# Ranking edges with one node range and a fifth of the edges on each partition, in a graph layer on one core

## The reference

```
edge_in = concatenate([h[row], h[col], dist], axis=1)
e   = silu(silu(edge_in @ eW1 + eb1) @ eW2 + eb2)
agg = segment_sum(e, row, num_segments=h.shape[0])
out = silu(concatenate([h, agg], axis=1) @ nW1 + nb1) @ nW2 + nb2
x   = layernorm(x + out)
```

## Time and profile before

| | |
|---|---|
| median of 3 runs | 629.42 us (627.53 to 630.96) |
| the profiled execution | 630.7 us, of which the span from the first to the last instruction is 628.9 us |
| busy: PE / PEld / DVE / ACT / POOL | 533.6 / 449.0 / 462.9 / 355.5 / 430.5 us |
| mean granted TensorE clock | 0.960 of full speed |

### The profile page before, as it was taken

The page is one execution under the profiler, slowest core; times in us unless marked ns, Lnnn a source line. Parts: engine busy times, 40 slices in busy tenths (PEclk is TensorE's granted clock), DMA queues, the critical chain, the costliest instruction groups (busy, mean ns, idle before and its releaser), DMA issues.

```text
span 628.9 us, 15166 instructions
## 1 busy us (share of the span) xinstructions
PE 533.6 (85%) x4653; PEld 449.0 (71%) x4653; DVE 462.9 (74%) x1364; ACT 355.5 (57%) x812; POOL 430.5 (68%) x465
## 2 busy tenths in 40 slices
PE   3953979779889979999998899889997888879695
PEld 2432768758768868887787788778776777769584
DVE  5998999988999898999788868797642533223356
ACT  4852555535645656665555555565556666556464
POOL 2327677566777777777777777777777777777750
PEclk9985889879989999999999999999999999999998
DMA  5121111111211112212121112111221212111111
GB/s 121 58 63 53 48 51 53 39 46 48 56 52 52 53 51 56 55 49 55 53 56 52 55 51 58 53 54 51 56 53 55 56 52 55 52 55 56 52 39 51
DMA packets 17215, 34.17 MB, mean 54 GB/s; under 512 B 8133, under 2 KB 9352, under 8 KB 17142
## 3 DMA queue, kind: packets, MB, share of 16 engines
q0 software_dynamic: 14080, 28.86, 16.8%
q1 hardware_dynamic: 2594, 3.40, 2.1%
q10 hardware_dynamic: 468, 0.96, 0.6%
HBM read 30.73 MB, written 2.40 MB: 53 GB/s over the span
## 4 chain that ended last, share of the span: by engine, by line
POOL 33%; DVE 27%; PE 18%; issue 16%; DMA 4%; DVEq 2%; ACTq 0%; SPq 0%
POOL q_rows L738 33%; PE layer_ps L751 7%; PE sort_ps L751 5%; PE seg_ps L751 4%; DVE load_hot L1215 3%; DVE agg L1286 3%; DMA q_rows<-q_table,q_index 3%; DVE hot L1271 2%; DVE count L1061 2%; DVE place L1105 2%; DVE col_hot L1209 1%; DVE row_hot L1210 1%; DMA x_sb<-in_x_dram 1%; DVEq L1278 1%; DVE slot L1111 1%
## 5 line engine op out<-in xcount | busy, mean ns | idle before, releaser
L738 POOL DMA_INDIRECT q_rows<-q_table,q_index x440 | 420.8, 956 | 155.0 <-issue 128.5
L585 ACT ACTIVATE e<-layer_ps 128x512 f32<-128x512 f32 x110 | 65.7, 597 | 212.5 <-PE seg_ps L751 207.4
L1286 DVE TENSOR_TENSOR agg<-agg,seg_ps 128x125 f32 x416 | 93.1, 280 | 95.2 <-PE seg_ps L751 92.0
L751 PE MATMUL layer_ps<-hotT,p_table 128*128 128x128 bf16 x1320 | 160.0, 225 | 0.1
L751 PE MATMUL layer_ps<-ident_f,q_rows 128*128 128x128 f32 x440 | 127.1, 289 | 34.7 <-DMA q_rows<-q_table,q_index 34.2
L751 PE MATMUL seg_ps<-hot,e 128*128 128x125 f32 x880 | 124.6, 285 | 19.4 <-DVE agg L1286 19.3
L751 PEld LDWEIGHTS layer_ps<-hotT,p_table 128*128 x1320 | 122.8, 99 | 23.6 <-issue 2.3
L751 PEld LDWEIGHTS seg_ps<-hot,e 128*128 128x128 f32 x880 | 109.0, 195 | 22.5 <-issue 20.3
L751 PE MATMUL layer_ps<-w_sb,h 128*128 128x128 f32 x880 | 120.0, 280 | 0.0
L751 PEld LDWEIGHTS layer_ps<-w_sb,h 128*128 128x128 f32 x880 | 111.6, 194 | 4.7 <-issue 0.2
L751 PEld LDWEIGHTS layer_ps<-ident_f,q_rows 128*128 128x128 f32 x440 | 63.3, 144 | 45.6 <-DMA q_rows<-q_table,q_index 43.8
(11 more groups left out here) (193 smaller groups left out, 432.1 us busy)
## 6 DMA issues: line engine op xcount, KB each, us to landing
q_rows<-q_table,q_index POOLq DMA_INDIRECT x440
q_table<-q_in_sb SPq DMA_DIRECT2D x1, 784.0 KB
x_sb<-in_x_dram ACTq DMA_DIRECT2D x1, 700.0 KB
q_table<-q_in_sb SPq DMA_DIRECT2D x1, 616.0 KB
out_dram<-x_sb SPq DMA_DIRECT2D x2, 224.0 KB
out_dram<-x_sb SPq DMA_DIRECT2D x1, 252.0 KB
w_in<-in_edge_weight_dram SPq DMA_DIRECT2D x1, 185.9 KB
dst_i<-in_dst_dram SPq DMA_DIRECT2D x1, 185.9 KB
```

Source lines behind the costliest of these rows:

```text
L585: A.activation(e2[:, m % 2, :], e_of(m)[:], ACT.Silu).then_inc(e2_ready, 1)
L738: P.indirect_dma_start(q_rows[:, g % RING, j, :], None, q_table, bass.IndirectOffsetOnAxis(ap=q_index[:, GT * g + j:GT * g + j + 1], axis= ...
L751: return nc.tensor.matmul(o, lhsT, rhs, start=start, stop=stop, **kw)
L1286: D.tensor_tensor(o, o, seg_ps[:, j * LO:(j + 1) * LO], ALU.add).then_inc(agg_added, 1)
```

## The change

The comparison of all 25 windows with every column on every partition goes. A partition now stands for one window and one fifth (a segment) of the edge columns of the chunk: 25 x 5 = 125 partitions. To bring the window numbers there, TensorE turns a chunk's numbers (`turn_windows`) and spreads them (`spread_windows`: one bf16 matmul of 125 x 125 per five columns, in up to three fills of four, four and two); ScalarE copies the spread to SBUF (`copy_spread`), except for chunk 0, where VectorE reads it in PSUM. `MATCH` is then one comparison with a number per partition, `SCAN` one scan over (columns / 5) x 125 elements with f32 results, `TOTAL` one instruction. `OFFSET` on VectorE gains two small instructions (`own`, `base_col`), `SUM` becomes two instructions in two halves, and `pick` on TensorE brings the places back to the edges (one f32 matmul per five columns, 125 x 125 weights, 5 columns moved). `SLOTS` reads them in PSUM and waits for `pick` and, from chunk 1 on, for TensorE's `DEST`.

The chunks become multiples of five columns, and `plan()` is written anew for them.

```diff
-LOAD = [50, 30, 38, 44, 48, 54, 54, 54, 53]
+SEG = 5
+LOAD = [50, 30, 45, 50, 50, 50, 50, 50, 50]
...
-    at(VECTOR, 9, (READ, 2, 0), (MATCH, 3, 0), (SCAN, 3, 0), (SCAN, 3, 1), (TOTAL, 3, 0))
+    at(VECTOR, 9, (READ, 2, 0), (MATCH, 3, 0), (SCAN, 3, 0), (TOTAL, 3, 0))
...
-    sorts(3, [12, 12, 13, 13, 14, 15, 15, 16], [13, 13, 14, 14, 15, 16, 16, 16])
+    sorts(3, [11, 12, 12, 13, 13, 14, 15, 15, 16], [12, 13, 13, 14, 14, 15, 16, 16, 17])
...
+            act.wait_ge(ident_ready, 2)
+            A.activation(column_sel[:], ident_b[0:NMAX, 0:NMAX].unsqueeze(2).to_broadcast([NMAX, NMAX, WIN]), ACT.Copy) \
+                .then_inc(column_sel_ready, 1)
...
+            def spread_windows(k, i):
...
+                sel = column_sel[:].rearrange("q c b -> q (c b)")
+                for t0, n, bank in spread_columns(k, i):
+                    for t in range(n):
+                        last = mm(bank[:, t, :], sel[0:LOAD[k], (t0 + t) * EP:(t0 + t + 1) * EP], win_t[0:LOAD[k], k, :], True, True)
+                last.then_inc(spread_made, 1)
+
+            def pick(k):
+
+                n = segments(k)
+                for t in range(n):
+                    if t in (0, n // 2):
+                        pe.wait_ge(place_ready, 2 * k + 1 + (t > 0))
+                    last = mm(slot_ps[k % 2][:, t * SEG:(t + 1) * SEG], count[:, t * EP:(t + 1) * EP], seg_sel[:], True, True)
+                last.then_inc(slots_ready, 1)
...
+                    half = segments(k) // 2 * EP
+                    for a, b in ((0, half), (half, wide)):
+                        D.scalar_tensor_tensor(count[:, a:b], count[:, a:b], base_col[:, 0:1], in_win[:, a:b],
+                                               ALU.add, ALU.mult).then_inc(place_ready, 1)
```

More of the change, by code:

```diff
@@ L64 @@
 TAG = 1 << 29
[L65 removed]
+assert sum(LOAD) == ECOL and TILES % GT == 0 and all(n % SEG == 0 for n in LOAD) and SEG * WIN == EP and V * CMAX <= 512
 assert all(EP * COL0[k] // SLOT + FULL[k] <= TABLE for k in range(CHUNKS)) and EP * max(LOAD) + SLOT <= 8000
@@ L77, in batches @@
     return [(a, min(BATCH, LOAD[k] - a)) for a in range(0, LOAD[k], BATCH)]
-MATCH, SCAN, TOTAL, OFFSET, SUM, SLOTS, DEST, WINDOW, SORT, READ, CARRY, CLOSE, ENCODE, NODE_X, RESIDUAL, CARRIED = (
-    "match", "scan", "total", "offset", "sum", "slots", "dest", "window", "sort", "read", "carry", "close", "encode",
-    "node_x", "residual", "carried")
+SPREAD, MATCH, SCAN, TOTAL, OFFSET, SUM, PICK, SLOTS, DEST, WINDOW, SORT, READ, CARRY, CLOSE, ENCODE, NODE_X, RESIDUAL, CARRIED = (
+    "spread", "match", "scan", "total", "offset", "sum", "pick", "slots", "dest", "window", "sort", "read", "carry", "close",
+    "encode", "node_x", "residual", "carried")
 VECTOR, TENSOR = {}, {}
@@ L131, in plan @@
[L131 to L141, removed]
@@ L142, in plan @@
-    at(VECTOR, 28, (READ, 4, 0))
+    sorts(3, [11, 12, 12, 13, 13, 14, 15, 15, 16], [12, 13, 13, 14, 14, 15, 16, 16, 17])
+    at(TENSOR, 15, (SPREAD, 4, 0))
+    at(TENSOR, 16, (SPREAD, 4, 1))
+    at(TENSOR, 17, (CLOSE, 3, 0), (SPREAD, 4, 2))
+    at(VECTOR, 18, (READ, 3, 0), (MATCH, 4, 0))
+    at(VECTOR, 19, (SCAN, 4, 0), (TOTAL, 4, 0))
+    at(TENSOR, 19, (OFFSET, 4, 0))
+    at(VECTOR, 20, (OFFSET, 4, 0), (SUM, 4, 0))
+    at(TENSOR, 20, (PICK, 4, 0), (DEST, 4, 0))
+    at(VECTOR, 21, (SLOTS, 4, 0), (DEST, 4, 0))
@@ L944, in _ @@
                     part(OFFSET, 1, 0)
+                    pick(1)
+                    part(DEST, 1, 0)
+                    part(WINDOW, 1, 0)
+                    spread_windows(2, 0)
                 first = first_layer(m)
@@ L955, in _ @@
                     last.then_inc(step_ready, 1)
-                if m == 0:
-                    part(DEST, 1, 0)
-                    part(WINDOW, 1, 0)
                 for name, k, i in TENSOR.get(m, ()):
@@ L1071, in part @@
+                    done(scanned[k])
+                    then(D.tensor_copy(one, ones[0:EP, 0:1]))
+                    scanned[k] = mark(D.tensor_tensor_scan(
+                        count[:, 0:wide], one.to_broadcast([EP, wide]), in_win[:, 0:wide], 0.0, ALU.mult, ALU.add))
+                elif name == TOTAL:
+                    done(scanned[k])
+                    D.tensor_scalar(total[:], win_sel[:], count[:, wide - 1:wide], None, ALU.mult).then_inc(totals_ready, 1)
                 elif name == OFFSET:
@@ L1353, in _ @@
             encode(*CODED[0])
-            for name, i in ((OFFSET, 0), (SUM, 0), (SUM, 1), (SLOTS, 0)):
+            for name, i in ((OFFSET, 0), (SUM, 0), (SLOTS, 0)):
                 part(name, 0, i)
@@ L1365, in _ @@
             dve.wait_ge(rest_coded, 2)
-            for name, i in ((ENCODE, 0), (MATCH, 0), (SCAN, 0), (SCAN, 1), (TOTAL, 0), (OFFSET, 0), (SUM, 0), (DEST, 0), (SUM, 1),
-                            (SLOTS, 0), (WINDOW, 0)):
+            for name, i in ((MATCH, 0), (SCAN, 0), (TOTAL, 0), (ENCODE, 0), (OFFSET, 0), (SUM, 0), (SLOTS, 0), (DEST, 0),
+                            (WINDOW, 0)):
                 part(name, 1, i)
```

235 lines of the change are left out of this document (153 added, 82 removed).

## The result

| | before | after |
|---|---|---|
| median of 4 runs | 629.07 us (627.53 to 630.96) | 638.69 us (635.15 to 639.54) |
| the profiled execution, its span | 630.7, 628.9 us | 635.15, 633.2 us |
| the first gather starts, the last gather starts | 41.48, 606.53 us | 48.20, 611.47 us |
| busy PE / DVE | 533.6 / 462.9 us | 563.4 / 426.1 us |

The ratio is 1.0143 (1.0103 to 1.0184): the change costs 1.4%, and the time lies above the predicted range. The profiled execution is the fastest of the runs; the other three took 638.6 to 639.5, and an unchanged copy of the kernel was profiled at 641.22. I read both, because what sets them apart is part of the answer.

What follows compares the result with a forecast made beforehand. GpSimd's 440 gathers (549 us) were taken to bound the kernel, plus first-gather start, waits, slow gathers and tail. Changes 5.3 + 2.0 - 6.1 = +1.2 on 629.4 gave 630.6 us; range 623 to 637.

Steps and rivals of the forecast that it cites:

- The queue order of the prologue: Before the first gather: chunk 0's `pick` ends about 20.2 us, with `pq(1)` queued behind it, making table work 5.1 late.
- the price of the rank: VectorE's rank instructions fall from 0.20 to 0.10 us a column, near 5 us in chunks of 50.
- a wait of some 3 us at group 3: GpSimd's thirteenth gather waits 3.4 us for TensorE's step 0; the 1.4 wait at 68.74 goes: +2.0.
- no waits behind 230 us: GpSimd's waits on TensorE's steps end by 196 us, with none later.
- late matmuls that cost nothing: From 292 us, `pick` and spread add 3.6 us a chunk, covered by TensorE's 5.5 us free.
- VectorE is late there by what its work sums to.: Stage to 196 us: VectorE's summed work sets GpSimd's waits on TensorE's steps, 3.7 in place of 9.8: -6.1.
- the relief: VectorE's cheaper rank shrinks GpSimd's waits up to 196 us, -6.1; as a rival, all 3.7 left also go: 625.3, chance 0.29.
- +5.3: Prologue: VectorE's `READ` comes 5.3 us later than 40.40, and the first gather starts at 46.8.
- The prologue costs more: Rival, chance 0.16: TensorE at its lower clock level before the first gather, 633.1 to 634.5; decided by `READ` over 7.2 later.
- Against it: from 13.7 on TensorE works without a gap: Argument against the dearer-prologue rival: TensorE, idle until 13.7 us, then works without a gap.
- the held gathers: Rival, chance 0.14: VectorE's `SUM` and comparison passes hold GpSimd's gathers, 10 to 12 us in place of 5.4: 635 to 637.

## Why the prediction was wrong

**Right.** The queue order of the prologue (`pick` to 20.36, forecast 20.2; `pq(1)` right behind), the price of the rank, a wait of some 3 us at group 3 (4.55 over the gap), no waits behind 230 us, late matmuls that cost nothing. Also right was that group 3's wait is paid out of the later ones: the two edits that remove it move most of it.

**The step that failed first: "VectorE is late there by what its work sums to."** I took VectorE's saving, 3.3, off the 10.0 us of waiting, and added 0.4 for TensorE. The stretch 68 to 230 us before the change:

```profile
68.00:230.00 162.00, 140.31 (x1289) 122.06 (x1287) 148.96 (x447) 90.44 (x206) 114.99 (x120) 0.95 0.18 50
```

The same stretch after the change, and behind it that of 292 to 500:

```profile
68.00:230.00 162.00, 150.77 (x1374) 129.32 (x1373) 137.86 (x399) 94.24 (x215) 117.65 (x123) 0.97 0.20 51
292.00:500.00 208.00, 196.29 (x1753) 168.07 (x1751) 142.30 (x427) 122.47 (x280) 157.72 (x166) 0.98 0.21 54
```

What TensorE stands waiting for VectorE in the stretch (total us, times, longest; waits below 1 us in all are left out), before and then after:

```profile
PE seg_ps L751 <- DVE agg L1286: 14.9, 10, 4.4
PE sort_ps L751 <- DVE total L1069: 5.0, 3, 3.2
```

```profile
PE seg_ps L812 <- DVE agg L1402: 3.7, 5, 1.7
PE sort_ps L812 <- DVE total L1186: 3.0, 3, 2.4
PE sort_ps L812 <- DVE count L1223: 2.9, 3, 1.1
PE sort_ps L812 <- DVE load_hot L1331: 1.7, 3, 0.8
```

Before the change TensorE was busy 140.31 us and VectorE 148.96 of these 162; now it is 150.77 and 137.86. VectorE lost 11.1 and TensorE gained 10.5: `pick` 7.0 for 29 matmuls, the spread 4.2 and the sorts of the added columns 4.9, less 4.9 of the matmuls of layers, turns and sums, of which the stretch holds a few fewer, and 0.7 of smaller ones and overlap. All of the 21.7 us that TensorE had free were waits for VectorE. They fell to 11.3, as the relief was to do, and TensorE's own added work filled what they left, so in this execution GpSimd waits about as long as before.

I had the price in hand, but set it against TensorE's slack only from 292 us on, and called it nothing. In chunks 2 to 4 it is 29 x 0.36 = 10.4 us. The hand-overs were priced too low as well: TensorE stands 2.9 us in `pick` for `count`, where I had added 0.4, and VectorE stands 3.2 ahead of `SLOTS` for `pick` and `DEST`, for which chunks 2 to 4 had no term. All waits from the first gather to 230 us, group 3 among them, were 11.2 before, were to be 7.1, and came to 11.6 and 14.5. The doubled matmuls show that there the time of `pick` and spread counts nearly in full, and that VectorE's still counts by some 0.6. How much of that is a full TensorE and how much the hand-over, and what the two additions would cost with the kernel before as base, stays open.

**The second: the size of +5.3.** It was counted with `pick` alone at a doubtful clock and the slots behind it as before. With the slots at the 1.2 GHz level it became 6.7 and 9.1. "The prologue costs more" named this and put 634.5 as its end, 2.5 to 3.9 more; it decided at 7.2, and the executions lie on both sides. "Against it: from 13.7 on TensorE works without a gap" was no argument, since the level also fell behind `pick` with TensorE busy throughout. That rival alone would have stayed within the range; with the missing relief it did not.

**The fallen rival.** Of the held gathers nothing is left in the sum: all gathers take 418.9 us, and over 0.944 each that is 3.5 in place of 5.4. The longest beside `SUM` takes 1.52 in place of 0.94 (292.63). In each of the chunks 2 to 8 one gather beside `SUM`, the pass with two inputs, was lengthened, in six of them by 0.29 to 0.58 us and in one by 0.05. Those beside `MATCH` were lengthened by 0.10 at most, but one beside two other scalar comparisons (`ge` and `dest_hot`, at 93.39) by 0.28. The Trainium skill ("SBUF — State Buffer", "Who interferes with whom") has a scalar comparison out of SBUF into SBUF as what can block, and a pass with two SBUF inputs as colliding with GpSimd's reads alone. The gather reads its index, `q_index`, out of SBUF, so the trace is in line with both, and I was wrong to read the rule as naming the new comparison only. What it bears on is 2 us.

**Open.** Why the full clock comes early in one profiled execution and late in the other was not settled, nor whether most of the spread from 633.6 to 641.2 us goes with it. Nor why the waits on TensorE's steps were 7.0 in one and 10.0 in another; the granted clock from 68 to 230 us was 0.97 and 0.93.

## What to carry to other kernels

When work moves from the engine that is late to another, put both engines' busy time and their waits for each other in that very stage side by side, before and after: the gain ends where the second engine's added work fills what the first one's relief sets free. A price that is hidden in a late stage has to be costed again in each early one. A wait that a ring of buffers merely brings forward is not worth removing, and before a small matmul is put ahead of a row of long ones, ask what is queued behind it.

## What the runs showed of the hardware

I had not expected a granted clock that falls while TensorE is busy all the time. In the execution of 641.22 us `pick` stands again at 300.62, and the clock of the stretches around it is:

```profile
300.62 2.37 PE L812 MATMUL sort_ps<-seg_sel,count 125*125 125x5 f32 x20
```

```profile
299.00:302.00 3.00, 3.00 (x32) 2.93 (x31) 1.41 (x6) 1.12 (x5) 2.11 (x3) 1.00 0.18 44
302.00:305.00 3.00, 3.00 (x19) 2.95 (x20) 1.01 (x6) 2.38 (x6) 2.36 (x3) 0.60 0.25 64
305.00:308.00 3.00, 3.00 (x24) 2.75 (x23) 1.99 (x10) 0.00 (x0) 2.39 (x3) 0.50 0.21 56
308.00:312.00 4.00, 4.00 (x33) 3.68 (x31) 2.08 (x8) 2.15 (x5) 3.00 (x4) 0.82 0.19 49
```

TensorE is busy for all 13 us, and behind the ten matmuls of 5 columns the clock goes from 1.00 to 0.50 and comes back. The kernel before, without `pick`, has 1.00 over 292 to 500 us, the changed one 0.98. There it costs nothing, as GpSimd has no wait behind 230 us; in the prologue, where every slot waits for TensorE, it does. Two by two between wider matmuls the ten of chunk 0 left the clock at 1.00 (20 to 22 us of that run). From 12 to 26 us of the 641.22 execution the view of stretches gives 1.00 while the pair that takes 1.02 elsewhere takes 2.05, so there I went by durations.
